# Four up products and four down products in a row instead of two and two, from unit 9 of each chunk

## What is computed

```python
def ffn(x):                      # D = 128, 64 experts of F = 64, top 8, plus one shared expert
    shared = silu(x @ Ws_up) @ Ws_down
    aff = x @ centroids.T
    idx = top_k(aff + biases, 8)
    w = sigmoid(aff[idx]); w = w / (w.sum() + 1e-8)      # scattered into cw, zero elsewhere
    h = silu(einsum('td,edf->etf', x, W_up))
    return shared + einsum('etd,te->td', einsum('etf,efd->etd', h, W_down), cw)

x = x + 0.5 * ffn(layernorm(x))
x = x + softmax(q @ k.T) / sqrt(128) @ v                 # q, k, v from layernorm(x)
x = x + 0.5 * ffn(layernorm(x))
```

## Time and profile before

| | |
|---|---|
| time, median of 3 runs | 545.74 us (545.43 to 548.09) |
| profiled execution's own time | 545.78 us, of which its span 544.0 us |
| TensorE busy in the span | 533.0 us (98%) |
| VectorE, ScalarE, GpSimd busy | 407.0 us (75%), 407.3 us (75%), 274.0 us (50%) |

### The profile page before, as it was taken

The page is one execution under the profiler, slowest core; times in us unless marked ns, Lnnn a source line. Parts: engine busy times, 40 slices in busy tenths (PEclk is TensorE's granted clock), DMA queues, the critical chain, the costliest instruction groups (busy, mean ns, idle before and its releaser), DMA issues.

```text
span 544.0 us, 8636 instructions
## 1 busy us (share of the span) xinstructions
PE 533.0 (98%) x2679; PEld 435.0 (80%) x2679; DVE 407.0 (75%) x926; ACT 407.3 (75%) x814; POOL 274.0 (50%) x242
## 2 busy tenths in 40 slices
PE   8899999999999999999999999999999999999997
PEld 5577887887888887699999999777887888788885
DVE  5989679877976676767777889778677867866564
ACT  6899778877887776766666667678778777877774
POOL 3579767775776763000000000166675776766663
PEclk9999999999999999999999999999999999999999
DMA  7676565554565540000000000055555565656562
GB/s 259 182 215 194 184 195 161 179 189 159 173 187 196 189 157 1 1 1 1 1 2 1 1 1 1 16 195 168 174 202 159 175 194 179 176 166 201 198 189 92
DMA packets 44270, 72.25 MB, mean 133 GB/s; under 512 B 8864, under 2 KB 9632, under 8 KB 44224
## 3 DMA queue, kind: packets, MB, share of 16 engines
q1 hardware_dynamic: 43568, 71.17, 41.9%
q10 hardware_dynamic: 592, 0.39, 0.2%
q0 software_dynamic: 64, 0.13, 0.1%
HBM read 69.57 MB, written 2.10 MB: 132 GB/s over the span
## 4 chain that ended last, share of the span: by engine, by line
PE 88%; DVE 6%; ACT 2%; issue 2%; DMA 1%; SPq 0%; DVEq 0%
PE lrow L1064 13%; PE lrow L1065 13%; PE lrow L1066 13%; PE bank L1102 11%; PE bank L1104 11%; PE bank L1103 11%; PE bank L1136 6%; PE bank L1348 3%; PE bank L1350 2%; PE bank L1349 2%; DVE pmax L879 1%; PE bank L1143 1%; PE bank L1064 1%; PE bank L1065 1%; PE bank L1066 1%
## 5 line engine op out<-in xcount | busy, mean ns | idle before, releaser
L277 POOL TENSOR_TENSOR gpart_lo<-gated,gpart_hi 128x512 fp32r<-128x512 f32 x174 | 224.0, 1296 | 164.2 <-ACT gpart_hi L442 162.5
L431 ACT ACTIVATE lrow<-lrow 128x512 f32<-128x512 f32 (+1 forms) x246 | 144.4, 587 | 63.9 <-PE lrow L1066 63.5
L678 DVE TENSOR_TENSOR gated<-lrow,wide 128x512 f32<-128x512 f32 x170 | 116.3, 684 | 57.6 <-ACT lrow L431 56.3
L442 ACT CAST gpart_hi<-gated 128x512 fp32r<-128x512 f32 x174 | 106.7, 613 | 5.7 <-DVE gated L678 5.1
L1102 PE MATMUL bank<-gpart_lo,wdn_hi 128*128 128x512 f32 x256 | 101.7, 397 | 0.0
L1104 PE MATMUL bank<-gpart_hi,wdn_hi 128*128 128x512 f32 x256 | 101.4, 396 | 0.0
L1103 PE MATMUL bank<-gpart_hi,wdn_lo 128*128 128x512 f32 x256 | 101.1, 395 | 0.0
L678 DVE TENSOR_TENSOR lrow<-lrow,wide 128x512 f32<-128x512 f32 x74 | 51.5, 696 | 28.0 <-ACT lrow L431 28.0
L997 DVE TENSOR_TENSOR pT_lo<-bank,pT_hi 128x512 fp32r<-128x512 f32 x64 | 43.8, 685 | 24.2 <-ACT pT_hi L618 24.2
L277 DVE TENSOR_TENSOR gpart_lo<-lrow,gpart_hi 128x512 fp32r<-128x512 f32 (+1 forms) x84 | 57.3, 682 | 1.8 <-ACT gpart_hi L442 1.3
L1102 PEld LDWEIGHTS bank<-gpart_lo,wdn_hi 128*128 128x128 f32 x256 | 48.0, 188 | 11.8
(11 more groups left out here) (246 smaller groups left out, 944.2 us busy)
## 6 DMA issues: line engine op xcount, KB each, us to landing
wide<-gates_dram SPq DMA_DIRECT2D x488, 128.0 KB, 3.0
raw<-in_w_up SPq DMA_DIRECT2D x8, 256.0 KB, 6.1
raw<-in_w_down SPq DMA_DIRECT2D x8, 256.0 KB, 6.3
gates_dram<-gates SPq DMA_DIRECT2D x8, 128.0 KB, 2.3
x<-in_x SPq DMA_DIRECT2D x3, 256.0 KB, 3.7
out_dram<-x SPq DMA_DIRECT2D x3, 256.0 KB, 3.0
x<-in_x SPq DMA_DIRECT2D x1, 128.0 KB, 2.7
x<-in_x ACTq DMA_DIRECT2D x1, 128.0 KB, 2.9
```

Of the source, the lines that this page charges most:

```text
L277: return eng.tensor_tensor(gpart[1][0:m, U % NGP, :], gated_at(U)[0:m, :], gpart[0][0:m, U % NGP, :].bitcast(F32), ALU.subtract)
L431: nc.scalar.activation(dst[0:m, :], hid[U % NH][0:m, :], ACT.Silu).then_inc(s_silu, 1)
L442: nc.scalar.copy(gpart[0][0:m, U % NGP, :], gated_at(U)[0:m, :]).then_inc(s_ghi, 1)
L678: nc.vector.tensor_tensor(gated_at(U), a, b, ALU.mult).then_inc(s_gated, 1)
```

## The change

From unit 9 on, TensorE's list issues up u, u+1, u+2, u+3 together when u is 9, 13, 17, 21, 25 or 29. The down products stay at their steps, so four of them follow: up 9 to 12, down 4 to 7, up 13 to 16, down 8 to 11, and so on to up 29 to 32, down 24 to 27. Units 7 and 8 stay a pair. The waits inside `up` and `down`, and everything on the other engines, are as before.

```diff
--- before.py
+++ after.py
@@ -1264,9 +1264,12 @@
                     for u in range(min(c, 1), UNITS):
                         if u <= EARLY and (c or u >= LEADS[f]):
                             up(u, n)
-                        if u > EARLY and u % 2 == 1:
+                        if u == EARLY + 1:
                             up(u, n)
                             up(u + 1, n)
+                        if u > EARLY + 2 and u % 4 == 1:
+                            for w in range(u, u + 4):
+                                up(w, n)
                         if n == 0 and u == 4:
                             spread_gate(3, n)
                         if n or u != 3:
```

## The result

The changed kernel takes 568.46 us (median, 567.97 to 569.03), the kernel before beside it 545.59: a ratio of 1.0411, 95% interval 1.0388 to 1.0435. The forecast was 569.0. The profiled execution took 568.65, its span is 566.9 (before: 544.0). In some executions, of the kernel before too, the mean granted clock is 0.991 to 0.997 in place of 0.999 or 1.00, and they are up to about 3 us longer (experiment 1: 562.94 at 0.993, the others 559.9 to 560.1), so where less than that decides, executions at 0.999 or 1.00 are compared.

What follows compares the result with a forecast made beforehand. TensorE, busy 98% of the span, was taken as the bound. Direct waits with restarts 17.98, the turn in five chunks 3.30 and in chunk 0 1.89 made 23.2 us on 545.78: 569.0, range 561 to 577.

Steps and rivals of the forecast that it cites:

- up 28, eight chunks: Up 28 waits for the low part of VectorE's unit 24, queued behind up 25's steps: 0.77 each, 6.16 us.
- up 16, chunks 1, 2: Up 16 waits for unit 12's low part, VectorE being later by the previous chunk's statistics: 1.39 each, 2.78 us.
- up 18, chunk 0: Behind the turn of the affinities, up 18 waits for the low part of VectorE's unit 14: 1.75 and a restart.
- up 20, chunks 1, 2, 4, 5, 6: Behind the turn of the affinities, up 20 waits for VectorE's gate 16: 0.56, with restart 0.66 each, 3.30 us.
- less the two waits of before: In chunk 0, the earlier kernel's waits at up 18 (0.35) and up 22 (0.29) are replaced; with restarts 0.84.
- the late turn: Turn of the affinities behind up 16's wait in six chunks, delaying VectorE's gate steps and later ups: 3.30 plus 1.89 us.
- What it put at nothing: Downs waiting for low parts, gate 16 behind the high part of 14, and gate slots behind transfers: no cost.
- Only direct waits: Rival: the turn's lateness is absorbed, leaving the waits for VectorE's fourth units: 561 to 563 us, chance 0.10.
- VectorE doesn't recover: Rival: VectorE, 2.3 behind after each turn, doesn't catch up before up 24: 577 us and over, chance 0.07.
- No wait, the count decides: Rival: each up keeps seven products of slack, so no up waits: 545.7 us, chance 0.03.
- Changes between up and down cost something: Rival: 96 fewer TensorE changes between up and down save time, under 1 us even at 0.01 each; chance 0.02.
- The clock falls in the gaps: Rival: four ups after each of 19 waits run at half clock, 53 us more: about 622, chance 0.03.

Runs made afterwards that it cites:

- experiment 1: The changed kernel with the turn of the affinities moved back behind up 14, fours kept: 560.02 us, ratio 1.0275.
- experiment 9: The changed kernel with seven buffers for the high and low parts in place of six: 569.19 us, ratio 1.0436.
- experiment 7: The changed kernel with units 12 and 24 of chunks 1 to 7 on GpSimd, 10 and 26 on VectorE: 557.16 us, ratio 1.0199.
- experiment 8: The changed kernel, fourth units on GpSimd in chunks 1 to 7, third and fourth in chunk 0, turn behind up 14: 546.96 us; control in pairs, same sharing: 547.21.
- experiment 2: The changed kernel with, on ScalarE's list only, the fourth unit's high part ahead of the next unit's SiLU: 577.43 us, ratio 1.0578.
- experiment 3: The changed kernel, fourth unit's high part ahead of the next SiLU (ScalarE) and low part ahead of the next gate step (VectorE): 557.17 us, ratio 1.0216.
- experiment 6: The changed kernel, high and low parts put first on both lists only for VectorE's fourth units, plus unit 8 in every chunk: 553.64 us, ratio 1.0147.

## Why the prediction was right, point by point

The step on which it rests held: seven products of distance in both orders, but the release of a VectorE unit hangs on the *next* unit's up, three products ahead of the up that needs the bank. The waits stand where they were named, 25 of them, and no other is over 0.15 that the kernel before doesn't have. By its terms (us, waits start to start; a restart is the second matmul's extra 0.10):

| term | predicted | measured |
|---|---|---|
| up 28, eight chunks | 8 x 0.77 = 6.16 | 0.76 to 0.77, 6.13 |
| up 16, chunks 0, 3 to 7 | 6 x 0.77 = 4.62 | 0.75 to 0.78, 4.59 |
| up 16, chunks 1, 2 | 2 x 1.39 = 2.78 | 1.37, 1.36: 2.73 |
| up 12 and up 24, chunk 0 | 0.98 + 0.77 | 0.88 + 0.76 |
| up 20, chunk 0 | 0.77 + 0.88 = 1.65 | 1.63 |
| up 18, chunk 0 | 1.75 | 1.41 |
| up 20, chunks 1, 2, 4, 5, 6 | 5 x 0.56 = 2.80 | 0.48 to 0.51, 2.46 |
| restarts | 25 x 0.10 = 2.50 | 25 x 0.104 = 2.60 |
| less the two waits of before | -0.84 | -0.85 |
| sum | 23.2 | 22.3 |

The spans differ by 22.9 and the medians by 22.87. Of what is over the rows' sum, 0.09 is a later start of unit 9 (26.81 against 26.72). The rest is at up 22 of chunks 1, 2, 4, 5 and 6, behind the late turn again: its second matmul comes 0.32 to 0.33 behind the first, as after a wait, though no idle time shows ahead of it. In the kernel before it comes 0.23 behind, and with the early turn (experiment 1) as well; five times the difference is 0.46. In chunk 5 of the changed kernel:

```profile
444.38 0.50 PE L1064 MATMUL lrow<-xnT_lo_b,wup_hi 128*128 128x512 f32 x1
444.72 0.39 PE L1065 MATMUL lrow<-xnT_hi_b,wup_lo 128*128 128x512 f32 x1
```

So the forecast of 569.0 is nearer than its terms: those that it named were 0.8 too long together, and it left out 0.55. That they cancel in part is luck.

*Up 18 of chunk 0* was sized 0.34 too long: the prediction carried over the 3.77 from L752 to the low part of 14, but in that stretch before the gate steps of 14 and 15 start 0.45 and 0.46 behind the step ahead of them, and when it comes late 0.34 and 0.28: 42.91 - 39.45 = 3.46 in all. *Up 20* was sized 0.06 to 0.08 too long: TensorE answers the gate step 0.68 after its start (440.09 - 439.41), not 0.75; the gate step is drawn with 0.63, the low part of the earlier trace rows with 0.69.

*What it put at nothing* was nothing: in the changed kernel no down product and no gate step shows a wait for a low part on GpSimd or for a DMA, and the seventh buffer gave nothing (experiment 9). One count on the way was wrong and did no harm: down 9 follows up 9 by ten products before, not twelve, so in the change the low parts of such units are older, not as old, and down 8 follows up 8 by fourteen, not sixteen (sixteen holds from unit 12 on). The attention stretch kept its length (up 29 of chunk 3 to up 1 of chunk 4: 144.55 before, 144.60 after).

*The rivals.* "Only direct waits" fell: the turn's wait at up 20 is there, and taking the turn forward gave 8.4 back (experiment 1). That is more than the 3.0 of the five waits at up 20 with their restarts. The turn, put between up 14 and up 15, is also work of TensorE that lies under the direct wait: its rows give 1.8 at up 16 in chunks 4 to 6 (from 0.77 to 0.19 each), 1.5 in chunks 1 and 2 (0.45 in brackets in place of 1.21) and 1.9 in chunk 0, 8.2 in all with the 3.0. "VectorE doesn't recover" fell: up 28 waits the same 0.61 in chunks with a turn and in chunks 3 and 7 without. "No wait, the count decides" fell with the first row, and experiment 7 shows why: the count is enough for GpSimd's units. The Trainium skill's page Perfetto Trace Analysis, section Matmuls, has groups rotate through PSUM banks so that one is evacuated under the matmuls of the next; experiment 8 agrees with it (546.96 against 547.21), and the changed kernel shows its limit: the evacuation was itself queued behind the next group. "Changes between up and down cost something" fell in experiment 8.

"The clock falls in the gaps" fell for the changed kernel: after the first slice PEclk shows 9 in all slices, with 25 gaps of 0.5 to 1.6 us among them. The sign that the prediction named, a granted clock under 1.00, did come (0.996 in the profiled execution), but ahead of the groups, where it cost nearly nothing (last section). The Trainium skill's page TensorE: Matmul & The Clock Gate, section "A second HAM failure mode: psum-queue depth-cycling", describes a clock that swings with short idles between groups. No run here shows a swing; experiment 2 shows a single fall behind its longest gap (last section).

## What to carry to other kernels

Count the time of a buffer not in products between its uses, but from the event that its release hangs on: here the consumer stood on two in-order lists behind the next item's steps, so a group of four gave the last of each group three products where the count said seven. When a group is made larger, look at its last member, and give it to the engine whose release comes first, or move its step ahead on *every* list it passes. A step put first on an in-order list holds all that is behind it while it waits, so put it first only where its input is sure to be there (557.1 in experiment 3 against 553.4 in experiment 6, at the same clock).

## What the runs showed of the hardware

The lower clock level came, in the changed kernel not in the gaps. Busy time in stretches of the changed kernel (columns as in the earlier trace rows):

```profile
5.00:9.00 4.00, 3.67 (x18) 2.17 (x18) 2.30 (x8) 3.82 (x10) 0.54 (x1) 1.00 0.99 292
9.00:13.00 4.00, 4.00 (x14) 3.00 (x14) 3.02 (x17) 3.33 (x7) 1.17 (x2) 0.57 1.06 404
13.00:17.00 4.00, 3.76 (x19) 2.69 (x17) 3.87 (x11) 3.70 (x8) 2.13 (x2) 1.00 0.43 158
```

and of experiment 2:

```profile
17.00:20.80 3.80, 2.67 (x8) 1.04 (x6) 3.71 (x12) 2.84 (x6) 3.08 (x4) 1.00 0.38 103
22.00:26.00 4.00, 4.00 (x10) 2.80 (x9) 3.77 (x11) 2.15 (x5) 1.06 (x2) 0.50 0.79 236
48.00:51.50 3.50, 1.28 (x7) 1.05 (x7) 2.83 (x14) 2.96 (x6) 2.14 (x2) 1.00 0.40 129
51.50:55.00 3.50, 3.50 (x11) 2.89 (x10) 2.09 (x4) 1.68 (x4) 2.03 (x3) 0.51 0.60 203
```

In each a few microseconds ran at the lower level (1.2 GHz, 0.50 of full): matmuls of 512 columns come 0.43 apart in place of 0.23. In the changed kernel it fell on the work up to 13 us; behind that TensorE idles in the kernel before (0.87 ahead of 14.44), and this idle time is gone, so unit 4 starts only 0.11 later and unit 9 0.09. In experiment 2 it fell first on units that nothing behind absorbs, and up 12 comes 2.7 later (32.68 against 29.96). It fell a second time at 51.5, right behind the longest wait of that kernel, 2.22 in brackets ahead of up 20 at 50.23: from up 20 to up 21 it is 5.50 there, 3.95 in the changed kernel. Ahead of the three TensorE was busy 92% (5 to 9), 70% (17 to 20.8) and 37% (48 to 51.5). But the kernel before was busy 74% at 16 us without a fall, and the changed kernel 45% from 43 to 46.7, with gaps of 1.24 and 1.47, without one:

```profile
43.00:46.70 3.70, 1.67 (x6) 1.05 (x6) 3.70 (x10) 3.52 (x8) 2.52 (x2) 1.00 0.43 122
```

So what sets it off is not settled here.
